# Later shift steps and a reordered GpSimd queue in the closing loop of a Mamba-2 and mixture-of-experts layer

## What is computed

```
x = x + layernorm(mamba2(layernorm(x)))
x = x + layernorm(ffn(layernorm(x)))

layernorm(v) = (v - mean(v)) / sqrt(var(v) + 1e-5)
ffn(x) = sum of the 8 chosen experts' outputs, weighted     (64 experts, 128 slots each)
       + (silu(x Wg) * (x Wu)) Wd * sigmoid(x w)            (shared expert, width 512)
```

## Time and profile before

| quantity | value |
|---|---|
| time before, median of 3 | 1446.54 us (1445.92 to 1451.17) |
| profiled execution: time | 1445.25 us |
| profiled execution: span | 1443.5 us |
| busy share of the span: PE, DVE, ACT, POOL | 86%, 72%, 64%, 58% |
| closing loop with its last stores | about 1312 to 1443.5 us |

### The profile page before, as it was taken

One profiled execution on the slowest core, in us unless ns is written; L12 is line 12 of the kernel. 1 busy time (PEld: TensorE's weight loads), 2 busy tenths in 40 slices (PEclk: granted clock), 3 DMA queues, 4 the chain that ended last, 5 costly groups with the idle time before them and its releaser, 6 DMA issues. The chain is left out here.

```text
span 1443.5 us, 27240 instructions
## 1 busy us (share of the span) xinstructions
PE 1235.3 (86%) x8578; PEld 1076.0 (75%) x8578; DVE 1033.6 (72%) x3118; ACT 927.6 (64%) x2106; POOL 842.4 (58%) x1017
## 2 busy tenths in 40 slices
PE   2899999999999999999999999729999999998950
PEld 2677778777777877877777787519999899998950
DVE  3788989989988998998899899544444434433763
ACT  2677887787788788778778877534444434444443
POOL 0356556656656655665665566516766667773566
PEclk9899999999999999999999999859999999999975
DMA  5500011001001001100100000056776677665554
GB/s 166 181 1 30 25 34 40 24 29 38 28 24 40 31 24 33 38 24 25 38 31 24 25 32 17 34 142 174 183 176 163 164 176 168 164 159 123 167 168 160
DMA packets 112934, 119.90 MB, mean 83 GB/s; under 512 B 19888, under 2 KB 99056, under 8 KB 112880
## 3 DMA queue, kind: packets, MB, share of 16 engines
q1 hardware_dynamic: 97744, 94.58, 20.8%
q0 software_dynamic: 14336, 23.08, 8.5%
q10 hardware_dynamic: 800, 1.57, 0.3%
HBM read 70.63 MB, written 48.56 MB: 83 GB/s over the span
## 5 line engine op out<-in xcount | busy, mean ns | idle before, releaser
L1025 POOL TENSOR_TENSOR mamba_arena<-mamba_arena 128x512 f32<-128x512 f32 (+2 forms) x384 | 382.8, 1007 | 300.3 <-DVE mamba_arena L804 202.7
L454 PE MATMUL bank<-identity,mamba_arena 128*128 128x128 f32 x704 | 112.4, 279 | 52.8 <-DVE mamba_arena L913 27.2
L804 DVE TENSOR_TENSOR mamba_arena<-bank,mamba_arena 128x512 f32<-128x512 f32 (+1 forms) x224 | 136.4, 610 | 16.0 <-PE bank L498 7.7
L454 PEld LDWEIGHTS bank<-identity,mamba_arena 128*128 128x128 f32 x704 | 84.9, 146 | 79.9 <-issue 27.2
L1370 PE MATMUL bank<-xt_hi,wsgu_hi 128*128 128x256 f32 x384 | 116.0, 302 | 22.3 <-DVE xt_lo L1753 13.8
L1370 PE MATMUL bank<-xt_lo,wsgu_hi 128*128 128x256 f32 x384 | 111.5, 290 | 0.0
L1370 PE MATMUL bank<-xt_hi,wsgu_lo 128*128 128x256 f32 x384 | 111.3, 290 | 0.0
L662 ACT ACTIVATE mamba_arena<-bank 128x512 f32<-128x512 f32 x192 | 100.2, 539 | 10.0 <-PE bank L454 7.5
L1370 PEld LDWEIGHTS bank<-xt_hi,wsgu_hi 128*128 128x128 f32 x384 | 76.5, 199 | 23.8 <-DVE xt_lo L1753 14.5
L804 DVE TENSOR_TENSOR mamba_arena<-mamba_arena 128x512 f32<-128x512 f32 (+1 forms) x128 | 54.7, 427 | 48.7 <-ACT mamba_arena L662 46.5
L666 ACT ACTIVATE mamba_arena<-x_all,mamba_arena 128x256 f32 (+1 forms) x128 | 69.9, 595 | 21.2 <-DVE mamba_arena L850 15.3
(11 more groups left out here) (367 smaller groups left out, 4476.3 us busy)
## 6 DMA issues: line engine op xcount, KB each, us to landing
experts_arena<-in_egu SPq DMA_DIRECT2D x64, 256.0 KB, 3.8
routed_sum<-zeros SPq DMA_DIRECT2D x1, 8320.0 KB, 27.0
x_all<-in_x SPq DMA_DIRECT2D x32, 256.0 KB, 2.7
token_table<-mamba_arena SPq DMA_DIRECT2D x64, 128.0 KB, 1.7
normed_transposed<-mamba_arena SPq DMA_DIRECT2D x32, 256.0 KB, 2.0
experts_arena<-normed_transposed SPq DMA_DIRECT2D x32, 256.0 KB, 3.7
experts_arena<-in_edown SPq DMA_DIRECT2D x64, 128.0 KB, 3.1
experts_arena<-routed_sum SPq DMA_DIRECT2D x32, 256.0 KB, 3.3
```

The costliest lines, as they stand in the source:

```text
L454: return nc.tensor.transpose(out, in_, identity[:, :])
L804: return nc.vector.tensor_tensor(out, a, b, op)
L1025: return nc.gpsimd.tensor_tensor(out, a, b, op)
```

## The change

The arithmetic and the number of compute instructions stay the same; places in three engines' lists change. VectorE's list takes the two shifts of step n-1 from the start of pass n and puts them behind the first five pieces of pass n (sum k = 0, statistics k = 1, products 0 and 1, statistics k = 0). ScalarE's norms k = 1 and 3 move behind the second high-part copy, k = 2 and 0 behind the third. GpSimd's list is now: stored sums of steps 0 and 1, and then for each step n both powers, four x sums, and the stored sums of step n+2 while n+2 < 5.

```diff
 # ScalarE, pass n (t = n + LEAD)
-                    if 0 < n:
-                        v = (n - 1) % 2
-                        eng.wait_ge(f_shift123, n)
-                        for b in range(NB):
-                            last = nc.scalar.activation(f_sum[:, v, 1, b, :], ...)
-                        last.then_inc(f_normed1, 1)
...
                         copy(act_hi[t % 2][:, 1], act_s[:, t % 2, 1]).then_inc(m_act_high1, 1)
                     if 0 < n:
                         v = (n - 1) % 2
-                        eng.wait_ge(f_shift0, n)
...
+                        eng.wait_ge(f_shift123, n)
+                        for b in range(NB):
+                            last = nc.scalar.activation(f_sum[:, v, 1, b, :], ...)
+                        last.then_inc(f_normed1, 1)
...
 # VectorE, pass n
-                    if 0 < n:
-                        eng.wait_ge(f_scale123, n)
-                        nc.vector.scalar_tensor_tensor(fshift[:, u, 1:4], ...).then_inc(f_shift123, 1)
-                        eng.wait_ge(f_scale0, n)
-                        nc.vector.scalar_tensor_tensor(fshift[:, u, 0], ...).then_inc(f_shift0, 1)
                     if 0 <= n < 8:
...
                         last.then_inc(f_stats0, 1)
+                    if 0 < n:
+                        eng.wait_ge(f_scale123, n)
+                        nc.vector.scalar_tensor_tensor(fshift[:, u, 1:4], ...).then_inc(f_shift123, 1)
...
 # GpSimd
-                for n in range(9):
...
+                stored_sums(0)
+                stored_sums(1)
+                for n in range(8):
+                    v = n % 2
+                    eng.wait_ge(f_mean0, n + 1)
...
+                    eng.wait_ge(f_mean123, n + 1)
...
+                    eng.wait_ge(f_normed1, n + 1)
+                    x_now = of_step(x_all, 2 * n)
+                    nc.gpsimd.tensor_tensor(x_now, x_now, f_sum[:, v, 1], ALU.add).then_inc(f_ready1, 1)
...
+                    if n + 2 < 8 - LEAD:
+                        stored_sums(n + 2)
```

More of the change, by code:

```diff
@@ L1639, in _ @@
                         split_tile(t + 1)
+                    if t < 8:
+                        eng.wait_ge(m_up_done0, t + 9)
+                        nc.scalar.activation(silu_s[:, t % 2, 0], bank[1][:, 0:NB * P], ACT.Silu).then_inc(m_silu_ready0, 1)
+                        eng.wait_ge(m_up_done1, t + 9)
+                        nc.scalar.activation(silu_s[:, t % 2, 1], bank[2][:, 0:NB * P], ACT.Silu).then_inc(m_silu_ready1, 1)
+                        if t > 1:
+                            eng.wait_ge(m_down_done1, t + 7)
+                        eng.wait_ge(m_act_ready0, t + 9)
+                        copy(act_hi[t % 2][:, 0], act_s[:, t % 2, 0]).then_inc(m_act_high0, 1)
+                        eng.wait_ge(m_up_done2, t + 9)
+                        nc.scalar.activation(silu_s[:, t % 2, 2], bank[3][:, 0:NB * P], ACT.Silu).then_inc(m_silu_ready2, 1)
+                        eng.wait_ge(m_act_ready1, t + 9)
+                        copy(act_hi[t % 2][:, 1], act_s[:, t % 2, 1]).then_inc(m_act_high1, 1)
                     if 0 < n:
@@ L1651, in _ @@
                     if t < 8:
[L1652 to L1655, removed]
+                        eng.wait_ge(m_up_done3, t + 9)
+                        nc.scalar.activation(silu_s[:, t % 2, 3], bank[4][:, 0:NB * P], ACT.Silu).then_inc(m_silu_ready3, 1)
+                        eng.wait_ge(m_act_ready2, t + 9)
+                        copy(act_hi[t % 2][:, 2], act_s[:, t % 2, 2]).then_inc(m_act_high2, 1)
                     if 0 < n:
@@ L1660, in _ @@
                         last.then_inc(f_normed2, 1)
[L1661 to L1669, removed]
                     if 0 < n:
@@ new lines, in stored_sums @@
+                def stored_sums(n):
+                    eng.wait_ge(routed_loaded1, 16 * n + 16)
+                    if n > 1:
+                        eng.wait_ge(f_ready1, n - 1)
+                    nc.gpsimd.tensor_tensor(f_sum[:, n % 2, 1], routed[:, 1], shared[:, :, 2 * n, :], ALU.add).then_inc(f_added1, 1)
+                    eng.wait_ge(routed_loaded3, 16 * n + 16)
+                    if n > 1:
+                        eng.wait_ge(f_ready3, n - 1)
+                    nc.gpsimd.tensor_tensor(f_sum[:, n % 2, 3], routed[:, 3], shared[:, :, 2 * n + 1, :], ALU.add).then_inc(f_added3, 1)
```

63 lines of the change are left out of this document (21 added, 42 removed).

## The result

| quantity | before | after |
|---|---|---|
| time, median of 11 runs each | 1447.31 us | 1440.78 us |
| lowest to highest | 1444.72 to 1451.17 us | 1436.12 to 1442.88 us |
| span of the profiled execution | 1443.5 us | 1441.2 us |
| ratio, with its 95% interval | | 0.9944 (0.993 to 0.9959) |

The changed kernel is 0.56% faster, 8.1 us by the ratio and 6.5 by the medians. The spans of the two profiled executions differ by 2.3 us only. So the first thing to read is where in the span they differ.

The account below looks back on a forecast made before the run. A loop of waits between engines, none full, was taken to set the pace. Rounds -11.8 us and first shift +1.9 gave -9.9, a profiled execution of 1435.3, plus 1.3 to the median: 1436.5 us, range 1431 to 1443.

Parts of the forecast that it names:

- The sum of the loop: Closing loop: seven rounds 71.9 us against 83.7, -11.8, and the first shift's +1.9, together -9.9 us.
- First shift +1.9: Start of the closing loop: sum, statistics and two products come first, so the first shift starts 1.9 us later, at 1350.0.
- The rounds: Closing loop, from one first shift to the next: 12.0, 11.9, 11.3, 9.8, 9.1, 9.1, 8.7 us.
- GpSimd's chain: Shift, norm, x sums, stored sums, powers, next shift: 10.4 us with stored sums, 8.3 without, plus port losses.
- VectorE's chain: VectorE's work in a full pass, 8.1 us, plus its port waits; named as limit of rounds 2 and 4.
- next tile's low part 0.85: Round 2, VectorE: the tile split's wait beside GpSimd's sums, 0.85 us, last of five such waits.
- five port waits: Round 2, VectorE: sum k = 2 0.8, low parts 1, 2, 3 0.6, 0.8, 0.75, next tile's low part 0.85 us.
- The port: VectorE instructions with both inputs in SBUF wait until 0.95 us after GpSimd's running sum starts; GpSimd's next loses 0.44 or 0.16.
- Port cheap: Rival for the closing loop: no instruction waits for the port, rounds 66.8 us, -15.0, time 1431.5 us; chance 0.10.
- slower rival: GpSimd keeps the port between its sums: rounds 87.8 us, with first shift +6.0, time 1452.5 us; chance 0.05.
- Gain half lost: Rival: rounds with stored sums stay 12.9, late loads hold the last three at 9.5; -3.9 us, 1442.5 us; chance 0.15.
- port wait of low part 3: VectorE's third low part: later norms delay it by about 1.0 us, covered by the same instruction's port wait.

Follow-up runs that it names:

- GpSimd's order alone: The kernel before with only GpSimd's new list (powers, four x sums, stored sums two steps on); ratio to before 0.9958, 1442.87 us.
- the places alone: The changed kernel with GpSimd's old list, so only VectorE's shifts and ScalarE's norms have new places; ratio to before 0.997, 1446.07 us.
- gate moved: The changed kernel with the gate (L1829) moved from the end of VectorE's pass to ahead of the shifts; ratio to before 0.9944.
- port taken away: The changed kernel with one input of VectorE's two-SBUF-input instructions read from PSUM from pass 0 on, values wrong; ratio to before 0.9899.
- reordered kernel: The changed kernel with shifts behind the tile split, low parts last, norms ahead of SiLUs, GpSimd's powers 1-3 first; ratio to before 0.9932, 1439.5 us.

## Why the forecast was right, and where it was off

**The sum of the loop.** Forecast -9.9 us, measured -9.05 from mark to end, the same in four profiles of each within 0.1. The mechanism is the one forecast: the waits for powers, for the first SiLU and the shift's port wait lose their cause. Behind the first shift VectorE waits for powers twice (5.3 us in all) and for no SiLU, and the shifts take 0.14 to 0.17 us.

**First shift +1.9:** measured +1.84 in all four. With GpSimd's order alone it is +0.00 and with the places alone +3.06, so it comes from the shifts' new place, as worked out.

**The rounds:** forecast 12.0, 11.9, 11.3, 9.8, 9.1, 9.1, 8.7, measured 12.13, 12.01, 11.51, 9.91, 9.22, 9.23, 8.74. Each is 0.04 to 0.21 short, 0.85 in all. For the third the cause can be read: I had put GpSimd's chain at 11.3. Its last power ends at 1390.85 + 1.34 = 1392.19, 11.34 us after the shift, so that term is right. But VectorE's chain, which I did not add up for this round, comes by my terms to 8.1 - 0.6 and 2.95 for the sum and three low parts, 10.45. The gate's 0.9 was missing, and VectorE arrives at 1392.36, 11.51 us after the shift. That is the mis-sized term: "next tile's low part 0.85" should read "whoever stands there first, 0.9", at the end of pass 3 as well, where no tile split follows. The gate moved shows it. In round 2 the five port waits make 3.97 us (0.86, 0.63, 0.82, 0.76 and the gate's 0.90) where I had 3.8, and the work 8.04 where I had 8.1 (the terms that I gave for it add up to 8.2). In rounds 5 and 6 L1854 costs GpSimd's adding of epsilon 0.49 us (0.74 in place of 0.25), not 0.4. The rest I have not divided.

**The port:** right for four of the five waits of pass 2. Sum k = 2 takes 1.54 us (about 1.5 forecast); the low parts 1 to 3 lose 0.6, 0.8 and 0.75, as forecast. The fifth is the tile split, which loses nothing, since the gate in front of it does. "Port cheap" would have been -15.0 in the loop and 1431.5 us: taking it away gave rounds of 67.35 (forecast for that bound 66.8) and -14.5. Both the forecast and its bound were of the right size. The slower rival needed a GpSimd that keeps the port through a row of sums; in passes 2 to 7 L1894 got in behind the first x sum. "Gain half lost" needed rounds of 12.9 to stay and late loads; neither came, with the DMA share at 0.78 from 1400 to 1420 us.

What the forecast read from its rows about this wait also stands in the runs. With one operand from PSUM the sum k = 2 took 0.68 us in place of 1.54 and the low part 1 0.39 in place of 1.02 (port taken away), so the second input in SBUF made the difference. An x sum took 1.53 or 1.54 us behind the sum k = 2 and 1.27 behind low part 1, in place of 1.09. A product that reads one input from PSUM, and the statistics, took the same time with GpSimd idle (the kernel before, from 1353.98 to 1357.10 us) as under the x sum of 1372.77 in the changed kernel:

```profile
1355.72 0.41 DVE L1908 TENSOR_TENSOR counts<-bank,counts 128x256 f32<-128x256 f32 x1
1356.05 0.74 DVE L1912 BATCH_NORM_STATS2 experts_arena<-experts_arena 128x6 f32<-128x256 f32 x2
```

```profile
1373.01 0.41 DVE L1909 TENSOR_TENSOR counts<-bank,counts 128x256 f32<-128x256 f32 x1
1373.34 0.74 DVE L1913 BATCH_NORM_STATS2 experts_arena<-experts_arena 128x6 f32<-128x256 f32 x2
```

These are times alone. That two engines share a port is the author's name for what they show, and no run shows the port itself.

The forecast applied this to two-input instructions alone. The gate has one input in SBUF and took 1.05 us beside a stored sum, 0.15 beside a power.

**What hid the rest:** the wait for an x sum ahead of the sum k = 0 of steps 6 and 7 was forecast at 1.8 us and is 1.17, since the gate in front of it stands 0.68 longer; the total is 1.85. The last wait for powers is 4.45 (4.5 forecast), the only other one 0.89. The port wait of low part 3 really hides late norms: with the port taken away that instruction waits 0.82 us for ScalarE.

**The time:** forecast 1436.5, measured 1440.78. Of the 4.3 us, 0.9 are the loop's. 0.9 are the median of before, 1447.31 where the forecast stood on 1446.4. The rest, 2.5 us, is the difference between -9.05 in the loop and -6.5 in the medians; it lies ahead of the mark, where the start moves by 6 us between executions of the same code. The median alone would not have told the rivals apart: 1440.78 lies nearer to "gain half lost" (1442.5) than to the forecast. It is the loop that decides, -9.05 against -3.9 for that rival. The interval of the ratio (-10.1 to -5.9 us) holds the loop's -9.05.

## What to carry to other kernels

When two engines pass work to and fro, lay both lists out with their durations and take the longer chain for each round; here that gave each of seven rounds within 0.21 us. The wait beside GpSimd's sums belonged here to a place, not to an instruction (0.9 us of it passed from the gate to the tile split when the gate moved): list everything that stands beside the other engine's sums, the smallest instruction too, before one moves a single one. When an order is changed, go through the DMA queue with the new order as well, or the load of what now comes first arrives last (VectorE waited 9.3 us for it in the reordered kernel); and compare profiles from a mark behind which the code differs, not by their whole span.

## What the runs showed of the hardware

- An instruction of 128x2 with one SBUF input (TENSOR_SCALAR) took 1.05 us in a row of GpSimd sums of 128x512, 0.57 when the sum had been running for 0.54 us (port taken away, issued at 1369.17), and 0.15 beside a power (gate moved).
- A power of 128x2 did not hold up a VectorE subtraction that was issued 0.27 to 0.29 us behind it: the tile split took its plain 0.68 us in the kernel before (power at 1357.42, split at 1357.70) and in all four profiles of the changed one. The power lost some time itself, 0.87 or 0.88 us in place of 0.73, with a low part just ahead of it. In the first profile of the changed kernel alone it took 1.53 (L2028 at 1352.30, shown above), at the same distances within 0.02 us. What makes the difference isn't known. The same two instructions in the changed kernel's third profile:

```profile
1351.12 0.87 POOL L2028 TENSOR_TENSOR experts_arena<-experts_arena,minus_half 128x2 f32<-128x2 f32 x1
```

```profile
1351.39 0.68 DVE L1833 TENSOR_TENSOR xt_lo<-experts_arena,xt_hi 128x512 fp32r<-128x512 f32 x1
```

- TensorE's matmuls (128x256) started 0.12 us apart behind an idle time of 2.16 us, and 0.21 us apart behind one of 4.04 us (the kernel before, at 1365.07 and 1377.96). The granted clock was 1.00 from 1365.1 to 1371 us, 0.50 from 1378 to 1383 and 1.00 again from 1384 to 1388. In the changed kernel it was 0.50 from 1396 to 1404 us, behind an idle time of 7.60 us; its VectorE waited for no SiLU from 1357 us on.
- The start of the closing loop varied from 1326.55 to 1334.10 us over 14 profiles, more than most changes here bring. The expert loop with its indirect DMAs stands ahead of it. What makes the start vary hasn't been tested.
